# Moving a small transpose to another PSUM bank, with new waits, in the second attention stage of a two-layer gated cross-attention kernel

## The reference

```
x = x + tanh(g_xattn[0]) * attention(layernorm(x), ctx, ctx, layer 0 weights)
x = x + tanh(g_ffn[0])   * mixture_of_experts(layernorm(x))
x = x + tanh(g_xattn[1]) * masked_attention(layernorm(x), ctx, ctx, mask, layer 1 weights)
x = x + tanh(g_ffn[1])   * quantised_ffn(layernorm(x))
```

```
scores = einsum('bhqd,bhkd->bhqk', query, key_h) * scale
scores = where(mask == 0, -1e9, scores)
attn = softmax(scores)
x = einsum('bhqk,bhkd->bhqd', attn, value)
return x @ wo.T + bo
```

## Time and profile before

| | |
|---|---|
| three executions | 1952.86, 1955.2, 1958.1 us; median 1955.2 us |
| the profiled execution: its time | 1958.1 us |
| its span in the trace | 1956.3 us |
| mean granted clock of TensorE | 0.965 of full speed |
| PE busy in the span | 1732.0 us (89%) |
| DVE busy | 1408.1 us (72%) |
| ACT busy | 1149.3 us (59%) |
| attention of layer 1 | about 1258 to 1745 us of the span |

### The profile page before, as it was taken

One profiled execution on the slowest core, in us unless ns is written; L12 is line 12 of the kernel. 1 busy time (PEld: TensorE's weight loads), 2 busy tenths in 40 slices (PEclk: granted clock), 3 DMA queues, 4 the chain that ended last, 5 costly groups with the idle time before them and its releaser, 6 DMA issues.

```text
span 1956.3 us, 53909 instructions
## 1 busy us (share of the span) xinstructions
PE 1732.0 (89%) x20198; PEld 1372.8 (70%) x20208; DVE 1408.1 (72%) x4651; ACT 1149.3 (59%) x2347; POOL 568.1 (29%) x552
## 2 busy tenths in 40 slices
PE   5999999999999998588788888499999999978855
PEld 4888888888888887376667666377777777743334
DVE  4788887888888887365444443378888888859988
ACT  3666666666666664122222222378888888858875
POOL 1000000000000000388888888411112121111147
PEclk9999999999999999798999999799999999989989
DMA  3122212221222241688988887422222222203265
GB/s 98 46 66 62 66 61 70 69 66 62 64 67 62 67 121 53 173 219 200 222 208 209 211 207 171 95 67 78 67 78 67 77 70 75 67 26 149 110 234 197
DMA packets 194481, 214.04 MB, mean 109 GB/s; under 512 B 25584, under 2 KB 170352, under 8 KB 192048
## 3 DMA queue, kind: packets, MB, share of 16 engines
q1 hardware_dynamic: 169408, 171.97, 27.3%
q0 software_dynamic: 24816, 38.62, 10.9%
HBM read 125.63 MB, written 84.89 MB: 108 GB/s over the span
## 4 chain that ended last, share of the span: by engine, by line
PE 57%; DVE 19%; ACT 7%; issue 6%; DMA 5%; POOL 5%; SPq 1%; POOLq 0%; DVEq 0%; ACTq 0%
DVE mt L835 8%; PE tiles L379 7%; PE tiles L362 7%; PE bank L445 6%; ACT pt L608 6%; PE bank L524 6%; DMA xr<-token_rows,tid 4%; PE bank L408 3%; PE bank L476 3%; PE tiles L346 3%; PE bank L457 3%; PE bank L547 3%; DVE hmax L1714 2%; PE bank L1292 2%; POOL accumulator L1501 2%
## 5 line engine op out<-in xcount | busy, mean ns | idle before, releaser
L1973 POOL TENSOR_TENSOR rstd<-var,minus_half 128x2 f32<-128x2 f32 x139 | 96.9, 697 | 882.3 <-DVE var L914 869.3
L835 DVE TENSOR_REDUCE mt<-tiles 128x16 f32<-128x2048 f32 x128 | 293.5, 2293 | 69.0 <-PE tiles L362 69.0
L608 ACT ACTIVATE pt<-tiles 128x2048 f32<-128x2048 f32 x128 | 240.7, 1881 | 48.8 <-PE tiles L379 48.8
L1501 POOL DMA_INDIRECT accumulator<-ye,tid x128 | 206.0, 1610 | 47.3 <-issue 32.2
L1446 DVE TENSOR_SCALAR ye<-bank,xr 128x256 f32<-128x256 f32 x128 | 56.1, 480 | 197.2 <-PE bank L1336 163.0
L1486 POOL DMA_INDIRECT xr<-token_rows,tid x128 | 141.2, 1103 | 71.3 <-DVE within L1414 33.1
L445 PE MATMUL bank<-xt,w_q 128*128 128x128 f32 x1024 | 155.9, 286 | 0.9 <-ACT xt L616 0.9
L362 PE MATMUL tiles<-qkp 32*128 32x256 f32 x2048 | 149.1, 404 | 3.2 <-ACT qkp L630 3.0
L379 PE MATMUL tiles<-qm,qkp 32*128 32x128 f32 x4096 | 150.2, 283 | 1.4 <-DVE mt L835 1.4
L379 PEld LDWEIGHTS tiles<-qm,qkp 32*128 32x128 f32 x4096 | 125.8, 186 | 27.3 <-issue 24.6
L445 PEld LDWEIGHTS bank<-xt,w_q 128*128 128x128 f32 x1024 | 132.7, 196 | 14.7 <-issue 13.0
(11 more groups left out here) (246 smaller groups left out, 4103.5 us busy)
## 6 DMA issues: line engine op xcount, KB each, us to landing
keys_values<-res SPq DMA_DIRECT2D x64, 256.0 KB
cxax<-accumulator SPq DMA_DIRECT2D x128, 128.0 KB, 2.3
cxax<-keys_values SPq DMA_DIRECT2D x128, 128.0 KB, 2.5
hidden_away<-h_ring SPq DMA_DIRECT2D x8, 1536.0 KB, 5.0
token_rows<-pay SPq DMA_DIRECT2D x64, 160.0 KB, 1.8
pt<-in_expert_up SPq DMA_DIRECT2D x36, 256.0 KB
cxax<-in_ctx SPq DMA_DIRECT2D x64, 128.0 KB, 2.2
res<-in_x SPq DMA_DIRECT2D x64, 128.0 KB, 2.3
```

The lines of the kernel that those rows point to most:

```text
L608: nc.scalar.activation(pt[r % 2][:, :, :], tiles[:, :, :], ACT.Exp).then_inc(sem("exp_done"), 1)
L835: nc.vector.tensor_reduce(mt[:, :].rearrange("p (i n c) -> p i n c", i=RT, n=2 * KC)[:, :, :, 0], tiles[:, :, :].rearrange("p i (n k) -> p ...
L1501: nc.gpsimd.indirect_dma_start(out=acc[p][:, :], out_offset=bass.IndirectOffsetOnAxis(ap=tid[b % 8][:, h:h + 1], axis=0), in_=ye[r][:, h, ...
```

## The change

Only layer 1's code comes out differently. The transpose of `mt` and its two readers move from bank 4, columns 256 to 383, to bank 6, columns 0 to 127. For layer 0 both forms name bank 4, columns 0 to 127, and the same waits.

The waits of layer 1 follow the bank. `maxima_t` no longer waits for the input copy `xt_out` of sequence b+2 and waits for `x3_done` of b-3, that is for the `residual` of this same slot, which reads bank 6. `transposes` loses its wait for `qm_done`. `output`, the next writer of bank 6, gets one for `qm_done` of sequence b+2.

```diff
-        MAXC = (0, D)
...
                 else:
-                    pe.wait_ge(sem(sm("xt_out")), ahead(b, 3))
-                nc.tensor.transpose(bank[4][:, MAXC[L]:MAXC[L] + P], mt[:, :], ident[:, :]).then_inc(sem("mt_done"), 1)
+                    wait(pe, sm("x3_done"), b - 2)
+                bk = bank[4 if L == 0 else 6]
+                nc.tensor.transpose(bk[:, 0:P], mt[:, :], ident[:, :]).then_inc(sem("mt_done"), 1)
...
                     wait(pe, sm("xt_out"), b)
-                    pe.wait_ge(sem("qm_done"), first + max(b - 2, 0))
...
                 else:
+                    pe.wait_ge(sem("qm_done"), first + ahead(b, 3))
                     wait(pe, sm("x3_done"), b)
...
-                                                          bank[4][:, MAXC[L]:MAXC[L] + P].unsqueeze(1).broadcast_to([P, KC, P]),
+                                                          bank[4 if L == 0 else 6][:, 0:P].unsqueeze(1).broadcast_to([P, KC, P]),
```

## The result

The changed kernel takes 1977.84 us (median of 4 executions, 1976.33 to 1978.39) against 1954.03 us for the kernel before, timed beside it. The ratio is 1.012, with a 95% interval from 1.0098 to 1.0142. It is slower by 23.8 us, 19 to 28 us by the interval.

The account below looks back on a forecast made before the run. Layer 1 attention's ring of masks, scores, maximum and exponential, 7.47 us a slot, was taken as the bound. 61 slots x 0.35 us = 21.4 us, other parts 0, on the median 1955.2 gave 1976.6 us; range 1968 to 1983.

Parts of the forecast that it names:

- The ring of the earlier trace: Layer 1's attention: masks, scores, maximum, masks, transposed scores, exponential, then the next slot's masks; 7.47 us a slot.
- the tie at the exponential's end: PE ends the transpose of `mt` at 1502.65, the exponential ends at 1502.66 to 1502.67: PE has nothing to spare.
- The two waits taken away: `maxima_t` loses `xt_out`, `transposes` loses `qm_done`; both were satisfied over 2 us before in the slot studied: gain 0.
- The residual's place: `residual` ends 0.02 us after the exponential, 0.30 us after the transpose's old start, and keeps its place in the ring.
- 0.38 us from the residual's end to the masks: Release to masks on PE: 0.12 us to the transpose's load, 0.26 us on to the masks; 0.35 us a slot later.
- the single case at 1260: Layer 1 attention's first slot before: the wait at L393 came last, released at 1260.34, masks began at 1260.72.
- rival A: `maxima_t`'s `x3_done` wait is bound to the transpose's load: 0.29 us a slot, 17.7 us, 1972.9 us; chance 0.10.
- Rival B: The masks' loads slip in beside the transpose on PE: 14.0 us more, 1969.2 us; chance 0.07.
- Rival C: Later `shifted`, delayed `output`, or masks waiting for the transpose's end: 24 to 29 us, 1979 to 1984; chance 0.08.
- D: Not slower: the residual ends 0.36 us or more earlier, so `maxima_t`'s wait costs nothing, 1955 us; chance 0.05.
- E: Faster: PE was the bound, `transposes` and all behind it move up, at most 9.9 us won, 1945; chance 0.02.
- The number of slots: `maxima_t`'s new wait is paid from b = 3 to 63 in layer 1: 61 slots of 0.35 us.

Follow-up runs that it names:

- The memset in the kernel before: Idle 128x512 float32 memset on DVE between `head_norm` and `residual`, added to the kernel before: 7.47 us a slot, 1955.72 us; added to the changed kernel: 8.01 us, 1984.43 us.
- half an output: Changed kernel with one of the two matmuls of layer 1's output projection left out, so its result is wrong: 7.58 us a slot, 1960.47 us.
- the wait alone: Kernel before, transpose still in bank 4, with only `maxima_t`'s wait for `x3_done` added: 7.82 us a slot, 1974.56 us, ratio 1.0093.

## Why the prediction was right

The forecast was 1976.6 us, 21.4 us more than before, from 61 slots of 0.35 us. The measured median is 1977.84 us, and 23.8 us more than the kernel before.

- *What bounded the kernel before.* The ring of the earlier trace rows and the tie at the exponential's end held. The memset in the kernel before shows the same thing from the other side: DVE work ahead of the residual is free there.
- *What bounds the changed kernel.* The prediction expected the chain to keep its members, with the residual and the transpose added behind the exponential. This was wrong. The exponential left the chain (7% to 1%), and `heads_to_tokens`, `output` and the residual stand in its place. The price came out right all the same, as the prediction took the residual's place from the end of `scores_t` and not from the exponential. For the next step it matters: by this chain a shorter exponential would no longer shorten the slot, and an earlier residual does, as half an output shows. The first of these was not run.
- *The two waits taken away, the one that `output` gets, the bank.* All at 0. The added wait alone gives 7.47; leaving bank 4 for bank 5, with `transposes` also without its wait, gives 7.47.
- *The residual's place.* 1.90 us after the exponential's start in both kernels. It did not move with the longer slot, and nothing added up from slot to slot.
- *0.38 us from the residual's end to the masks.* Measured 0.38, as in the single case at 1260: 0.12 and 0.26. Naming the wait first gives 0.06 and 0.26. That was rival A, and as a kernel of its own it lands on its price: 7.76 us a slot, as worked out.
- *Rival B, mask loads beside the transpose.* In the changed kernel and in all five others in which small tiles follow this transpose at once, it is 0.26 us from its load to theirs (medians of 0.26 over 60 to 62 slots each). Turning the order round, masks first, doesn't avoid it. The Trainium skill (TensorEngine Tiling (Array Packing), section "Key Properties") says that a change of tiling mode drains TensorE. The rows are in line with it, though not to the letter: the load of L345 at 1500.46 comes 0.07 us ahead of the transpose's modelled end (1500.53).
- *Rival C.* L847 starts 2.39 us after the exponential's start in place of 2.29: the 0.1 us of the prediction. The maximum isn't late for it.
- *Rivals D and E.* Nothing was hidden and nothing won. Even with the residual 0.24 us earlier, in the kernel with half an output, 0.11 us a slot is left.
- *The number of slots.* 61 transposes waited for the residual, as predicted, but only 60 slots grew. Behind the last of these transposes come no masks of a next sequence, and the last two exponentials are 4.94 us apart in both traces. The prediction counted one slot too many, 0.35 us.
- *The range.* Its low end, 1968, lies 1.2 us below rival B's 1969.2. That is half of the spread of 2.3 us and not most of it; nothing hangs on this.

The sum over the stage is then 60 x (7.82 - 7.47) = 21.0 us. In the two profiled executions the stage from the first exponential to the last grew by less, from 470.8 to 490.5 us, or 19.7, since its first slot was 8.8 us in place of 10.1. That slot ran partly at the lower of TensorE's two levels in both, with a mean granted clock of 0.66 of full speed before and 0.81 after. The change is not the reason: among the ten profiled executions, five have a first slot of 10.0 to 10.2 us at 0.66 to 0.67 (the kernel before and four variants, the wait alone among them) and five one of 8.8 to 9.1 us at 0.81 (the changed kernel and four variants, bank 5 among them).

Kernel before:

```profile
1267.00:1277.00 10.00, 8.54 (x126) 6.26 (x126) 4.11 (x8) 5.54 (x12) 1.43 (x2) 0.66 0.08 26
```

Changed kernel:

```profile
1263.00:1272.00 9.00, 7.26 (x127) 5.15 (x126) 4.34 (x8) 5.88 (x12) 1.71 (x3) 0.81 0.13 37
```

The stages ahead were 3.6 us shorter in the execution after, so the two profiled executions differ by only 17 us. The distance of the medians, 23.8, is 2.8 us above the sum; the interval of 19 to 28 us holds the sum. The wait alone, with the same slot, came out at 18 us (13 to 23). I take the 2.8 us as scatter between executions; no part of the trace shows them. That the whole time came out within 1.2 us of the forecast is in part luck: the median of before turned out 1.2 us lower than the 1955.2 that the forecast starts from, and the difference 2.4 us larger than forecast. The slot, 7.82 us as predicted, is the firm part.

## What to carry to other kernels

A buffer's price is the wait for its last reader, and that is read in the slot where the new user stands: ask when the reader ends, not how much room the buffer has. Here bank 5 was free at that moment and bank 6 was 0.3 us too late. A step that waits in an engine's queue costs twice when the bound stands right behind it: for the wait (0.09 us here), and for its own time (0.26 us here), which was hidden and now is on the ring. Look in the profile for one odd place where the coming wait was already the last, as in a stage's first slot. Here its 0.38 us held in every slot, though it was read from a single one. Then ask which steps lead to the new wait: they, and no longer those of the old ring, set the next slot.

## What the runs showed of the hardware

- In `maxima_t` the wait named first is bound to the load, and the second one is a sequencer instruction of its own (51 ns in the trace). The first released the load 0.06 us after the residual's end, the second 0.12 us. Naming the wait that comes last first was worth 0.06 us in each of 60 slots.
- A 128x128 float32 transpose followed by small-tile matmuls held PE for 0.26 us from load to load (0.23 from matmul to matmul in the row at 1500.23), where two such transposes in a row (L425, L487) are 0.11 us apart.
- On DVE the residual started 0.08 us ahead of the recorded end of the instruction before it where its waits were already met (half an output, memset), and 0.03 us after PE's modelled end where it had to wait for `output`. This is not so of every DVE instruction: the memset, with a wait of its own, started 0.06 us after the end of `head_norm`.
